# Attention's preparation cut by feature blocks instead of token tiles, with the keys loaded one group earlier

## What is computed

```
def _layernorm(x, axis=-1, eps=1e-05):
    m = jnp.mean(x, axis=axis, keepdims=True)
    v = jnp.var(x, axis=axis, keepdims=True)
    return (x - m) / jnp.sqrt(v + eps)
...
    x = x + _L1_xattn_ref(_layernorm(x, axis=-1), ctx_512, ctx_512)
```

## Time and profile before

| | |
|---|---|
| median of 3 runs | 2109.56 us (2109.5 to 2125.61) |
| profiled execution | 2110.66 us, its span 2108.9 us |
| mean granted TensorE clock | 0.918 |
| busy share PE / DVE / ACT / POOL | 85% / 66% / 50% / 44% |
| attention | from about 1149 to about 1622 us of the span |

### The profile page before, as it was taken

One profiled execution on the slowest core, in us unless ns is written; L12 is line 12 of the kernel. 1 busy time (PEld: TensorE's weight loads), 2 busy tenths in 40 slices (PEclk: granted clock), 3 DMA queues, 4 the chain that ended last, 5 costly groups with the idle time before them and its releaser, 6 DMA issues. The chain is left out here.

```text
span 2108.9 us, 32488 instructions
## 1 busy us (share of the span) xinstructions
PE 1788.2 (85%) x9679; PEld 1016.9 (48%) x9679; DVE 1388.2 (66%) x2786; ACT 1059.5 (50%) x2135; POOL 918.2 (44%) x991
## 2 busy tenths in 40 slices
PE   4689877898447999999994599999996539999997
PEld 2344443444244555555552133333332538888885
DVE  5887877878585665655653687778783865455553
ACT  5588777888333333333331377777776512222222
POOL 5466676668203555555552241541111014444442
PEclk8699988999777999999997599999999759999999
DMA  5111121111354879989665643333222618999893
GB/s 150 56 41 41 57 84 61 41 41 41 128 168 103 178 185 237 232 181 232 146 116 102 121 124 72 89 87 82 64 58 62 252 49 228 232 233 236 229 233 65
DMA packets 194352, 270.93 MB, mean 128 GB/s; under 512 B 86956, under 2 KB 111500, under 8 KB 193164
## 3 DMA queue, kind: packets, MB, share of 16 engines
q1 hardware_dynamic: 150364, 168.23, 27.2%
q0 software_dynamic: 38544, 97.02, 22.5%
q10 hardware_dynamic: 5280, 3.67, 0.6%
HBM read 199.20 MB, written 69.17 MB: 127 GB/s over the span
## 5 line engine op out<-in xcount | busy, mean ns | idle before, releaser
L291 POOL TENSOR_TENSOR g_near<-g_mask,g_tb 128x512 f32<-128x512 f32 x256 | 322.2, 1279 | 99.8 <-DVE g_emin L545 98.8
L2096 DVE TENSOR_REDUCE a_negmax<-a_m 128x2 f32<-128x1024 f32 x256 | 304.3, 1221 | 85.6 <-PE a_m L1882 85.5
L1969 ACT ACTIVATE a_prob<-a_s 128x512 f32<-128x512 f32 x512 | 274.8, 595 | 90.6 <-PE a_s L1892 89.3
L1464 PE MATMUL f_gu_bank<-f_wgu,f_xT 128*128 x768 | 265.8, 489 | 2.9 <-ACT f_xT L1512 2.9
L1258 PEld LDWEIGHTS s_gu_bank<-s_xT,s_wgu 128*128 128x128 f32 x2048 | 240.3, 193 | 31.8 <-issue 27.5
L374 PE MATMUL g_pt<-g_ident,g_p 128*128 128x128 f32 x1024 | 173.7, 299 | 89.4 <-DVE g_pT L554 84.2
L1426 POOL DMA_INDIRECT out<-f_y,f_ids x96 | 151.7, 1580 | 209.7 <-DMA out<-f_y,f_ids 167.6
L1258 PE MATMUL s_gu_bank<-s_xT,s_wgu 128*128 128x128 f32 x2048 | 240.9, 276 | 1.6 <-ACT s_xT L1288 1.6
L475 ACT ACTIVATE g_p<-g_e,g_emin 128x512 f32<-128x512 f32 x256 | 183.4, 716 | 97.2 <-DVE g_emin L545 96.5
L374 PEld LDWEIGHTS g_pt<-g_ident,g_p 128*128 128x128 f32 x1024 | 122.3, 150 | 219.7 <-DVE g_pT L554 146.5
L1464 PEld LDWEIGHTS f_gu_bank<-f_wgu,f_xT 128*128 128x128 f32 x768 | 146.3, 191 | 126.1 <-issue 49.3
(11 more groups left out here) (296 smaller groups left out, 2766.3 us busy)
## 6 DMA issues: line engine op xcount, KB each, us to landing
s_wgu<-in_L_ffn_w_gate_up SPq DMA_DIRECT2D x32, 1024.0 KB
f_wgu<-in_L_ffn_gate_up_proj SPq DMA_DIRECT2D x32, 768.0 KB
s_wd<-in_L_ffn_w_down SPq DMA_DIRECT2D x32, 512.0 KB
g_tb<-neighbours SPq DMA_DIRECT2D x8, 1536.0 KB
f_wd<-in_L_ffn_down_proj SPq DMA_DIRECT2D x32, 384.0 KB
a_qT<-q_parts SPq DMA_DIRECT2D x64, 192.0 KB, 3.4
q_parts<-a_part SPq DMA_DIRECT2D x16, 384.0 KB, 4.0
g_tb<-neighbours SPq DMA_DIRECT2D x8, 512.0 KB
```

Of the source, the lines that this page charges most:

```text
L291: pool.tensor_tensor(near[:, n % LAG, :], mask[slot][:, local % NT, :], t_all[k % SLOTS][:, local // NT, :], ALU.add).then_inc(near_ready, 1)
L1464: last = nc.tensor.matmul(gu_bank[j % TR][:, 0:F], xT[j % TR][:, c, :], wgu_flat[:, bass.ds(place_of[j] + c * F, F)], start=(c == 0), stop ...
L1969: nc.scalar.activation(prob[n][:, :], bank_of("score", G, n)[:, :], ACT.Exp).then_inc(p_ready, 1)
L2096: V.tensor_reduce(negmax[k % RING][:, 2 * half:2 * half + 2, head], m_bank[i % RING][:, :, :], X_AXIS, ALU.max, negate=True).then_inc(m_re ...
```

## The change

A unit of queries becomes 128 features of all 512 tokens of a batch. Its parts serve two groups (unit c serves groups 2c and 2c + 1 of its batch). FIRST becomes 5: the keys of batch 0 and the four query units of batch 0. The late units are 15: for each of batches 1 to 3 the keys and four query units, in groups 0 to 4, 8 to 12 and 16 to 20. `load_q` waits only for its own unit. The normed tokens `xn` have two buffers, so the ACT norms no longer wait for the units of the batch before; POOL makes its eight norms as pairs after groups 7, 8, 13 and 14. A stored unit has rows of 512 contiguous bf16 elements, where it had runs of 128. SP stores the late unit at the start of its body, where it did so at the end, and loads the next batch's keys as 3, 3 and 2 pieces in the second to fourth group. The load of the tokens of batch 1 moves behind `store(0)` on SP, and the load of the context of batches 1 to 3 (768 KB) moves behind the first units on ACT.

```diff
-    units = [("keys", 0)] + [("tokens", t) for t in range(NT)] + [("keys", b) for b in range(1, B)]
+    units = [("keys", 0, 0)] + [("queries", 0, c) for c in range(DC)]
     FIRST = len(units)
-    units += [("tokens", t) for t in range(NT, TT)]
-    late_group = list(range(NT)) + list(range(KV, KV + 2 * NT))
+    for b in range(1, B):
+        units += [("keys", b, 0)] + [("queries", b, c) for c in range(DC)]
+    place_of = {unit: u for u, unit in enumerate(units)}
+    late_group = [G for G in range(GROUPS - KV) if G % KV <= DC]
+    norms_at = {7: (8, 9), 8: (10, 11), 13: (12, 13), 14: (14, 15)}
...
-        xn = sb("xn", [P, NT, D])
+        xn = sb("xn", [P, 2, NT, D])
-        part = sb("part", [P, PLACES, DC, PARTS, P], BF16)
+        part = sb("part", [P, PLACES, PARTS, N], BF16)
...
                 def load_q(G, k):
-                    if g == 0 and b > 0:
-                        for r in range(PLACES):
-                            sp.wait_ge(stored[r], 16 * (2 + b))
+                    if g % 2 == 0:
+                        u = place_of["queries", b, g // 2]
+                        sp.wait_ge(stored[u % PLACES], 16 * (u // PLACES + 1))
...
                 load_tokens(0, NT // 2, 0)
-                load_tokens(NT, NT, 2)
                 sp.wait_ge(consts, 4)
                 load_keys(0, len(K_PART))
-                for u in range(3):
-                    store(u)
+                store(0)
+                load_tokens(NT, NT, 2)
                 for r in range(len(K_PART)):
                     load_keys(0, r)
-                for u in range(3, 5):
-                    store(u)
-                for t in range(NT):
-                    sp.wait_ge(stored[(1 + t) % PLACES], 16 * ((1 + t) // PLACES + 1))
+                store(1)
                 load_q(0, 0)
                 load_q(1, 1)
-                for u in range(5, FIRST):
+                for u in range(2, FIRST):
                     store(u)
...
                 def body(G, k, ahead):
+                    if G in late_at:
+                        store(FIRST + late_at[G])
...
-                    if b < B and 0 <= step < 4:
-                        load_keys(b, 2 * step)
-                        load_keys(b, 2 * step + 1)
-                    if G in late_at:
-                        store(FIRST + late_at[G])
+                    if b < B and 0 <= step < 3:
+                        for r in range(3 * step, min(3 * step + 3, len(K_PART) + 1)):
+                            load_keys(b, r)
...
                 def turn(u, target):
+                    what, b, c = units[u]
+                    for t in range(NT):
+                        source = ctx_sb[:, b * NT + t, :] if what == "keys" else xn[:, b % 2, t, c * P:(c + 1) * P]
+                        last = nc.tensor.transpose(target[:, t * P:(t + 1) * P], source, ident[:, :])
...
-                act.dma_start(ctx_sb[:, NT:TT, :], ctx_dram[1:B, :, :].rearrange("b (t p) f -> p (b t) f", p=P)).then_inc(ctx_in[1], 16)
                 first_part(0)
...
                 second_part(FIRST - 1)
+                act.dma_start(ctx_sb[:, NT:TT, :], ctx_dram[1:B, :, :].rearrange("b (t p) f -> p (b t) f", p=P)).then_inc(ctx_in[1], 16)
...
-                    if G + 1 in late_at and late_at[G + 1] >= NT:
-                        norm(late_at[G + 1] + NT)
+                    for t in norms_at.get(G, ()):
+                        norm(t)
```

More of the change, by code:

```diff
@@ L1715, in part_of, with xn_of @@
         def part_of(u, j):
-            return part[:, u % PLACES, :, j, :]
+            return part[:, u % PLACES, j, :]
         def left_of(u):
-            return left[:, u % PLACES, :].rearrange("p (c s) -> p c s", c=DC)
+            return left[:, u % PLACES, :]
+        def xn_of(t):
+            return xn[:, t // NT % 2, t % NT, :]
         def by_head(row):
@@ L1744, in load_keys @@
                     if r == 0:
-                        sp.wait_ge(stored[b], 16 * 2 if b else 16)
+                        u = place_of["keys", b, 0]
+                        sp.wait_ge(stored[u % PLACES], 16 * (u // PLACES + 1))
                     if r < len(K_PART):
@@ L1753, in store @@
                 def store(u):
-                    what, i = units[u]
+                    what, b, c = units[u]
                     for j in range(PARTS):
                         sp.wait_ge(part_ready[j], u + 1)
[L1757 to L1761, removed]
+                    target = k_parts[b, :, :, :] if what == "keys" else q_parts[b, c, :, :, :]
+                    sp.dma_start(target.rearrange("j p s -> p j s"), part[:, u % PLACES, :, :]).then_inc(stored[u % PLACES], 16)
                 def load_tokens(first, count, s):
@@ L1844, in turn, with source_ready @@
                 def turn(u, target):
-                    what, i = units[u]
-                    for c in range(DC):
-                        if what == "keys":
-                            source = ctx_sb[:, i * NT + c, :]
-                        else:
-                            source = xn[:, i % NT, c * P:(c + 1) * P]
-                        last = nc.tensor.transpose(target[:, c * P:(c + 1) * P], source, ident[:, :])
-                    last.then_inc(unit_ps, 1)
-                def first_unit(u):
-                    what, i = units[u]
-                    if what == "keys":
-                        pe.wait_ge(ctx_in[min(i, 1)], 16)
-                    else:
-                        pe.wait_ge(xn_dve if i % 2 else xn_act, i // 2 + 1)
+                    what, b, c = units[u]
+                    for t in range(NT):
+                        source = ctx_sb[:, b * NT + t, :] if what == "keys" else xn[:, b % 2, t, c * P:(c + 1) * P]
+                        last = nc.tensor.transpose(target[:, t * P:(t + 1) * P], source, ident[:, :])
+                    last.then_inc(unit_ps, 1)
+                def source_ready(u):
+                    what, b, c = units[u]
+                    if what == "keys":
+                        pe.wait_ge(ctx_in[min(b, 1)], 16)
+                    elif b == 0:
+                        pe.wait_ge(xn_act, NT // 2)
+                        pe.wait_ge(xn_dve, NT // 2)
+                    elif b == 1:
+                        pe.wait_ge(xn_act, NT // 2 + NT)
+                    else:
+                        pe.wait_ge(xn_pool, (b - 1) * NT)
+                def first_unit(u):
+                    source_ready(u)
                     if u >= PLACES:
                         pe.wait_ge(left_ready, u - PLACES + 1)
-                    turn(u, unit_bank(u))
+                    turn(u, unit_bank(u % PLACES))
                 def late_unit(i):
-                    if i < NT:
-                        pe.wait_ge(xn_act, NT // 2 + i + 1)
-                    else:
-                        pe.wait_ge(xn_pool, i - NT + 1)
+                    source_ready(FIRST + i)
                     bank_free("unit", i)
@@ L2192, in all_parts @@
                     u = FIRST + i
-                    source = turned[i % RING][:, :].rearrange("p (c s) -> p c s", c=DC)
+                    source = turned[i % RING][:, :]
                     pool.wait_ge(turned_ready, i + 1)
```

16 lines of the change are left out of this document (7 added, 9 removed).

## The result

The changed kernel takes 2097.97 us in the median of 17 runs (2093.89 to 2109.22), the kernel before 2112.78 us in 17 runs (2107.25 to 2125.61). The ratio is 0.9926 with a 95% interval of 0.9911 to 0.9941, so 0.74% or 15.6 us less (the two medians differ by 14.8). Stages that the change doesn't touch differ by a few microseconds from execution to execution, so for parts I measure attention itself, from the first DMA issue of its tokens to the start of the last transposition of an output.

A forecast was written before the change was run, and what follows sets the result against it. PE sets the steady period, but waits 17.6 us for the first queries and three times for keys (2.98, 2.51, 2.75 us). Keys 13.1 + start 5.8 - late units 1.4 = 17.5 us less, forecast 2092 us, range 2086 to 2100.

The forecast's parts named there:

- forecast case: Whole kernel: the main outcome, a time of 2089 to 2095 us, chance 0.45.
- Keys one group earlier: Steady state: PE's three key waits go, giving 2.98 + 5.56 + 4.55, 13.1 us in sum, at least 8.2.
- Three more late units: Steady groups: 15 late units instead of 12, each costing 0.48 us, 1.4 us lost, bounds 0 to 2.9.
- POOL's norms in pairs: After groups 7, 8, 13 and 14: a second norm leaves POOL 2.3 us idle, cost 0, at most 1.29 us.
- The start: Before the first product: six steps let PE begin at 1179.5, 5.8 us earlier.
- Step 1: Start: lighter first loads move everything up to the norms 1.4 us sooner, bounds 0.9 and 2.
- Steps 4 and 5: Start: keys through at 1173.1, with 1.2 us added by the context load; the store of unit 1 lands at 1175.2.
- Step 6: End of the start: 4.3 us from the issue of the queries to the first product.
- The start gains more: Start: the store of unit 1 isn't behind all keys, lands about 1170.5; 10.5 us gained, time 2087.4, chance 0.2.
- The start gains little: Start: context load counts in full, 3 us gained; VectorE's statistics may take back key-wait excess; 2095 to 2098, chance 0.2.
- The clock stays: Key waits: the clock falls for another reason, only the idle 8.2 us come back; 12.6 in all, 2097, chance 0.08.
- The maxima are late: Groups 1 to 3, 9 to 11, 17 to 19: SP's fuller queue delays maxima rows, PE idles; 2133 or 2101, chance 0.04.

The follow-up runs named there:

- e1: The kernel before with only the next batch's keys loaded as 3, 3 and 2 pieces in groups 1 to 3; 2100.17 us, ratio 0.9913.
- e3: The changed kernel with ACT's context load of batches 1 to 3 issued behind the norms of batch 1; 2095.07 us, ratio 0.9889.
- e5: The kernel of e3 with the parts of a unit in runs of 256 bytes again; 2097.39 us, ratio 0.9932.
- e7_tokens_behind: The kernel of e3 with batch 1's tokens loaded behind the first queries, its statistics and norms moved between maxima of groups 0 and 1; 2095.53 us, ratio 0.9908.
- e11_all_three: The kernel of e7_tokens_behind with the keys of batch 0 in DRAM runs of 8 KB; 2094.90 us, ratio 0.9901.

## Why the prediction was right

The forecast was 17.5 us less and a time of 2092 us within 2086 to 2100; attention measured 15.4 us less, and the time is 2098. That is inside the range, but outside the 2089 to 2095 of the forecast case. Of the 6 us between 2092 and 2098, 3.2 are the base: the kernel before stood at 2109.56 in 3 runs and at 2112.78 in 17. The rest is the gain, 14.8 us between the medians and not 17.5. Most of the sum held. One term, the first key wait, had its mechanism wrong; the start came out right with two errors in it; and 0.6 us came in the interval of group 0 (16.20 for 16.79), which no term had.

*Keys one group earlier, 13.1 us.* Measured 10.5. The second and third places gave 5.56 and 4.55 us, exactly the excess I took, and e1 shows that the clock's part belongs to the wait. The first place gave 0.43 in the place of 2.98, and here the step that failed is the sentence "What is late next at that place? ... nothing that the trace shows". The trace did show it, and one of the prediction's own rivals names it: VectorE made its aggregates at 1285.6 to 1286.5 inside TensorE's wait, and they cost 0.9 us (13.30 - 12.40, the interval of a group with statistics) once it was gone. The other 1.65 us is the clock behind ScalarE's root. That wait of 1.7 us stood in the trace of before too, without a fall, and the prediction doesn't mention it. With the two terms, e1's 2.1 us (no fall) and the whole's 0.43 (fall) come out.

*Three more late units, 1.4 us.* Of the 15 groups with a late unit 14 have 12.70 to 12.74 us, and group 0 has 16.20; groups 13 to 15 and those from 21 on, without one, have 12.23. Taken over the affected groups it is 2.42 us for groups 16 to 20 and 0.30 for group 4, where statistics already stretched the interval, less 1.45 for groups 13 to 15: 1.27. The cover held.

*POOL's norms in pairs, 0.* No wait of TensorE for the maxima's split shows up in a steady group, and group 8 keeps 12.71. Held.

*The start, 5.8 us.* Measured 5.46. That this is within 0.4 us is in part luck, as two errors of 1.0 and 1.3 us cancel. Step 1 gave 0.7 us (the norms start at +10.74 for +11.42) and not 1.4, because the context tile of batch 0 was not quicker at all, and the keys' store went out 0.1 later, not 0.5 sooner. Steps 4 and 5 had the store land at +25.6; it did at +24.6, mainly since the context took nothing from the keys, for which step 4 had 1.2 us. Step 6 cost 5.64 us, not 4.3, and there the context's tail is (e3). This is one of the signs by which the prediction said that it would be wrong, the context load as a longer stretch before the first product; it came, and the number held all the same. The context's price of 1.3 to 2.2 us lies within the bounds of 0 and 2.1 or at their edge, with its place one step too early. The Trainium skill, page DMA: Bandwidth & Descriptors, section Issuing engines are not separate DMA queues, lets transfers of all issuing engines share the same 16 DMA engines and interleave. In 1173:1176 the trace agrees, with 0.54 MB of the context beside 0.38 MB of SP's queue. In 1169.6:1173 it does not: the context load was issued and moved nothing while the keys did.

*The rivals.* "The start gains more" did not come: the store landed at +24.6, behind the keys, and not at about +20.9. "The start gains little" did not come either, as the start gained 5.46 us and not 3, but its clause on VectorE's statistics did, and its 2095 to 2098 holds the measured time, by another sum than its own. "The clock stays" was wrong at its own two places, but something like it happened at the third, by another wait. "The maxima are late" did not happen: no wait of TensorE for those rows in the steady groups, and SP's query issue in its body of group 1 took 1.59 us where it took 5.14. The longer runs of the stores do this, as e5 has 5.30 us with short runs and e3 1.83 with long ones.

## What to carry to other kernels

When a wait of the bounding engine goes, list what the other engines did during it: small work that fitted there (here an aggregate of 0.8 us) comes out as the next wait. A wait costs its idle time and, where the clock falls behind it, 1.65 to 3.1 us more in these traces; so remove it as a whole interval, and look at the waits that stay, since a harmless one can turn into a dear one. In front of a long first transfer, order the queue by who needs the data first: a store that unblocks everything should not be behind megabytes that are needed a group later, on any issuing engine.

## What the runs showed of the hardware

A wait of TensorE of 1.71 us was followed by 1.2 GHz in four traces (the changed kernel twice, e7_tokens_behind and e11_all_three) and by 2.4 GHz in eight others, with the same work around it; both traces of the changed kernel had it. Loads that write 16 partitions each ran at 121 to 159 GB/s with the DMA engines busy when their runs were 1 KB, and at 139 when they were 8 KB; with a second queue for three of seven it was not more (160 GB/s for 174, the query store included). A store over 128 partitions had 288 GB/s and the token loads 368. A context load issued by ScalarE while SP's keys were moving moved nothing until they were through, for 3.4 us in the changed kernel. A store of 384 KB landed 3.6 us after its issue with runs of 256 bytes and 2.8 us with runs of 1024.
